# Attention stage of a four-layer kernel: context products issued in two halves around the next head's scores, and two projections of the fourth head group moved

## The reference, cut to what matters

```python
# layer 0 (A0)
scores = jnp.einsum('bkgld,bksd->bkgls', q, k) * scale
scores = scores + encoder_attention_mask[:, :, None, :, :]
attn = jax.nn.softmax(scores, axis=-1)
out = jnp.einsum('bkgls,bksd->bkgld', attn, v)
...
# layer 1 (A1 and A2)
scores = jnp.einsum('bhqd,bhkd->bhqk', q, k) / jnp.sqrt(jnp.float32(HD))
scores = scores * mask - 10000.0 * (1.0 - mask)
probs = jax.nn.softmax(scores, axis=-1)
return jnp.einsum('bhqk,bhkd->bhqd', probs, v)
```

## Time and profile before

| | us |
|---|---|
| median of 3 runs | 4186.95 |
| lowest and highest | 4186.92, 4193.72 |
| profiled execution, whole time | 4188.31 |
| its span in the trace | 4186.5 |
| span busy: PE, DVE, ACT, POOL | 89%, 63%, 51%, 39% |

### The profile page before, as it was taken

How to read it: one execution, slowest core, us unless ns; L and a number is a source line. 1 busy time by engine, 2 the same in 40 slices (tenths; PEclk the granted TensorE clock), 3 DMA queues, 4 the chain that set the end, 5 groups by cost and what they waited for, 6 DMA issues and landing times. The chain is left out here.

```text
span 4186.5 us, 66406 instructions
## 1 busy us (share of the span) xinstructions
PE 3719.4 (89%) x24448; PEld 2267.5 (54%) x24448; DVE 2621.0 (63%) x5691; ACT 2154.2 (51%) x4272; POOL 1652.4 (39%) x1849
## 2 busy tenths in 40 slices
PE   7988899899888989989888888998988888899898
PEld 4544565546554456554655445656465454565555
DVE  5765746666576564665657656467666765645766
ACT  5655733434666573343466657334346665733433
POOL 4554442232454454223245445422324544542232
PEclk9999999999999999999999999999999999999999
DMA  4032221102204122110220412211022032221102
GB/s 137 15 103 67 78 78 40 62 21 101 76 15 123 49 84 70 39 64 21 101 76 15 121 53 82 70 42 60 22 101 78 20 117 55 78 70 42 60 32 101
DMA packets 94558, 276.11 MB, mean 66 GB/s; under 512 B 25472, under 2 KB 25984, under 8 KB 73088
## 3 DMA queue, kind: packets, MB, share of 16 engines
q1 hardware_dynamic: 94208, 271.58, 20.2%
HBM read 201.24 MB, written 4.19 MB: 49 GB/s over the span
## 5 line engine op out<-in xcount | busy, mean ns | idle before, releaser
L805 POOL TENSOR_SCALAR probs<-probs,row_inv 128x512 f32<-128x512 f32 x1024 | 696.0, 696 | 635.1 <-DVE row_inv L720 635.1
L664 ACT ACTIVATE probs<-probs,row_max 128x512 f32<-128x512 f32 x1024 | 733.4, 725 | 132.1 <-DVE row_max L736 131.2
L559 PE MATMUL ps<-ident,probs 128*128 128x128 f32 x4096 | 606.5, 289 | 172.9 <-ACT pT L658 146.5
L559 PEld LDWEIGHTS ps<-ident,probs 128*128 128x128 f32 x4096 | 477.0, 146 | 383.0 <-ACT pT L658 211.4
L658 ACT ACTIVATE pT<-ps 128x512 f32<-128x512 f32 x768 | 430.1, 602 | 107.2 <-PE ps L559 106.5
L369 PE MATMUL ps<-mix,wring 128*128 128x512 f32 x1024 | 471.0, 596 | 3.8 <-DMA wring<-in_blocks_dram 3.8
L534 PE MATMUL ps<-kstack,qstack 96*128 96x512 f32 (+1 forms) x1024 | 380.5, 467 | 16.2 <-DMA qstack<-hi 7.1
L736 DVE CUSTOM_DVE_ANT_0 probs<-ps,maskA 128x512 f32<-128x512 f32 x512 | 329.3, 681 | 42.6 <-PE ps L534 42.6
L736 DVE CUSTOM_DVE_ANT_0 probs<-ps,neg 128x512 f32<-128x512 f32 x512 | 340.6, 685 | 8.9
L369 PEld LDWEIGHTS ps<-mix,wring 128*128 128x128 f32 x1024 | 191.2, 190 | 198.9 <-issue 178.8
L1535 POOL TENSOR_TENSOR hinv<-hvar,minus_half 128x32 f32<-128x32 f32 x24 | 146.3, 6094 | 376.8 <-DVE hvar L1255 376.8
(11 more groups left out here) (177 smaller groups left out, 7025.9 us busy)
## 6 DMA issues: line engine op xcount, KB each, us to landing
wring<-in_blocks_dram SPq DMA_DIRECT2D x151, 1024.0 KB, 5.1
qstack<-hi SPq DMA_DIRECT2D x256, 64.0 KB, 2.0
kstack<-hi SPq DMA_DIRECT2D x256, 64.0 KB, 2.0
maskA<-in_mask_dram SPq DMA_DIRECT2D x9, 1024.0 KB, 7.8
rows<-in_rows_dram SPq DMA_DIRECT2D x8, 1024.0 KB, 4.6
qstack<-hi SPq DMA_DIRECT2D x256, 32.0 KB, 2.0
qstack<-lo SPq DMA_DIRECT2D x128, 64.0 KB, 2.0
kstack<-lo SPq DMA_DIRECT2D x128, 64.0 KB, 2.0
```

The lines of the kernel that those rows point to most:

```text
L559: ins = nc.tensor.transpose(tile[:, qc * P:(qc + 1) * P], probs[:, m % PSLOTS, qc, kc * P:(kc + 1) * P], ident[:, :])
L664: nc.scalar.activation(p, p, ACT.Exp, bias=row_max[:, n % PSLOTS, qc:qc + 1], scale=-1.0, accum_out=row_sum[:, n % PSLOTS, qc:qc + 1]).the ...
L805: nc.gpsimd.tensor_scalar(p, p, row_inv[:, (n - 1) % PSLOTS, qc:qc + 1], 1.0, ALU.mult, ALU.mult)\
```

## The change

Three things are edited. The arithmetic stays the same.

1. In all three attentions a group's context products of key blocks 0 and 1 are issued one step earlier, behind the last transposes of the group's own last head. Those of key blocks 2 and 3 follow in the next step, behind its first scores and ahead of its transposes.
2. In A1 and A2 the query projection of group 3 moves from step 4 to steps 2 and 3, one matmul a half. It is written into bank 7, not into the ring. ACT's split of it moves to the end of step 3, POOL's with it.
3. In A1 and A2 the key projection of group 3 moves from step 5 to step 8, still in a ring bank. ACT's and POOL's splits of it move along.

The core of the diff:

```diff
+        IN_HEADS = {(0, 0): ('q', 2, (0, 1)), (0, 1): ('q', 2, (2, 3)), (1, 0): ('k', 2, (0, 1)), (1, 1): ('k', 2, (2, 3)),
+                    (2, 0): ('q', 3, (0,)), (2, 1): ('q', 3, (1,)), (3, 0): ('q', 3, (2,)), (3, 1): ('q', 3, (3,)),
+                    (8, 0): ('k', 3, (0, 1)), (8, 1): ('k', 3, (2, 3))}
+        SPLITS = {n: (kind, c) for (n, half), (kind, c, fcs) in IN_HEADS.items() if C - 1 in fcs}
...
-            tile = take(pe, 'q', A.tag, g) if tile is None else tile
+            if tile is None:
+                tile = ps[:, OBANK, :] if not A.shared and g == 3 else take(pe, 'q', A.tag, g)
...
+            def context(vg, kcs):
+
+                first, final = (vg % 2 == 0, vg % 2 == 1) if A.shared else (True, True)
+                for kc in kcs:
+                    if kc == 0:
+                        if vg == 0 and not A.shared:
+                            pe.wait_ge(*act_emptied.when('q', t, 3))
+                        if first and vg > 0:
+                            pe.wait_ge(*act_done.when('context', t, (vg // 2 if A.shared else vg) - 1))
+                        if vg == 0:
+                            for tc in range(C):
+                                pe.wait_ge(*dve_emptied.when('v', t, tc))
+                    for h in range(4):
+                        evac_wait(pe, ('pT', t, 4 * vg + h, kc))
+                    for h in range(4):
+                        lhs = v0[:, kc, vg, :] if A.shared else v1[:, kc, (4 * vg + h) * 32:(4 * vg + h + 1) * 32]
+                        ins = nc.tensor.matmul(ps[32 * h:32 * h + 32, OBANK, :], lhs, pT[:, h, kc, :],
+                                               start=(kc == 0 and first), stop=(kc == C - 1 and final))
+                    ins.then_inc(*S['context_ready'].reach(t, vg, kc))
...
-                    for kc in pair:
-                        if m >= 0 and mi == 0 and vg >= 0:
...
+                    if m >= 0 and mi == 0 and half == 0 and vg >= 0:
+                        context(vg, (2, 3))
...
-                    if not A.shared and g + 2 < A.groups and i < 2:
-                        part = (pe_q, pe_k)[i](pe, A, g + 2, fcs=(2 * half, 2 * half + 1), tile=None if half == 0 else part)
+                    if m >= 0 and mi == 3 and half == 1:
+                        context(mg, (0, 1))
+
+                    if not A.shared and (n, half) in IN_HEADS:
+                        kind, c, fcs = IN_HEADS[n, half]
+                        part = {'q': pe_q, 'k': pe_k}[kind](pe, A, c, fcs=fcs, tile=None if 0 in fcs else part)
...
+            bank = OBANK if label[0] == 'q' and not A.shared and g == 3 else ring.bank(*label)
...
-                    if step == 's' and not A.shared and g + 2 < A.groups and i < 2:
-                        act_split(act, A, 'qk'[i], g + 2)
+                    if step == 's' and not A.shared and n in SPLITS:
+                        act_split(act, A, *SPLITS[n])
...
+                if not A.shared and n - 2 in SPLITS:
+                    pool_split(pool, A, *SPLITS[n - 2])
```

More of the change, by code:

```diff
@@ L521, in pe_attention @@
                 vg = mg - 1
-                first, final = (vg % 2 == 0, vg % 2 == 1) if A.shared else (True, True)
                 if n < A.heads and i == 0:
@@ L536, in pe_attention @@
                                 .then_inc(*S['scores_ready'].reach(t, n, qc))
-                    for kc in pair:
-                        if m >= 0 and mi == 0 and vg >= 0:
-                            if kc == 0:
-                                if first and vg > 0:
-                                    pe.wait_ge(*act_done.when('context', t, (vg // 2 if A.shared else vg) - 1))
-                                if vg == 0:
-                                    for tc in range(C):
-                                        pe.wait_ge(*dve_emptied.when('v', t, tc))
-                            for h in range(4):
-                                evac_wait(pe, ('pT', t, 4 * vg + h, kc))
-                            for h in range(4):
-                                lhs = v0[:, kc, vg, :] if A.shared else v1[:, kc, (4 * vg + h) * 32:(4 * vg + h + 1) * 32]
-                                ins = nc.tensor.matmul(ps[32 * h:32 * h + 32, OBANK, :], lhs, pT[:, h, kc, :],
-                                                       start=(kc == 0 and first), stop=(kc == C - 1 and final))
-                            ins.then_inc(*S['context_ready'].reach(t, vg, kc))
+                    if m >= 0 and mi == 0 and half == 0 and vg >= 0:
+                        context(vg, (2, 3))
                     if 0 <= m < A.heads:
@@ L623, in act_split @@
             bias = scaled[:, t * C + g:t * C + g + 1] if kind == 'q' else col(A.bk, g)
-            nc.scalar.activation(split[:, s, :], ps[:, ring.bank(*label), :], ACT.Identity, bias=bias,
+            bank = OBANK if label[0] == 'q' and not A.shared and g == 3 else ring.bank(*label)
+            nc.scalar.activation(split[:, s, :], ps[:, bank, :], ACT.Identity, bias=bias,
                                  scale=A.scale if kind == 'q' else 1.0).then_inc(*act_emptied.reach(*label))
@@ L796, in pool_attention @@
                 g, i = divmod(n - 1, 4)
-                if not A.shared and g + 2 < A.groups:
-                    if i == 1:
-                        pool_split(pool, A, 'q', g + 2)
-                    if i == 2:
-                        pool_split(pool, A, 'k', g + 2)
+                if not A.shared and n - 2 in SPLITS:
+                    pool_split(pool, A, *SPLITS[n - 2])
                 for qc in range(C):
```

## The result

The changed kernel takes **4201.91 us** (median), the kernel before 4186.93 in the same rounds. The ratio is 1.0031, 95% interval 1.0021 to 1.004: slower by 15 us, where no change was forecast. The time lies inside the stated range (4168 to 4203), at its slow end. The profiled execution took 4201.91 us with a span of 4200.1, against a span of 4186.5 before.

What follows compares the result with a forecast made beforehand. No engine is full, so hand-over waits between engines bound the kernel. A0 +5.0, A1 and A2 -8.1, stack +1.6 sum to -1.5 us: 4185.4 median, forecast as no change, range 4168 to 4203.

Steps and rivals of the forecast that it cites:

- X + 6.04: A1 and A2: X starts ACT's copies in a group's last step; next head's copy follows a context at X + 6.04.
- A0, 7 x 4 groups at 0.18: A0's context steps: second copy 0.18 us later in each of 28 groups, +5.0 us in all.
- a run under 6.8: Sign against the forecast: a solid PE run in A0 shorter than 6.8 us means its idle time was reached.
- Chain, point 1: A1: ACT's copies of step 4 at 282.43, step 6 at 288.47, step 7 at 293.69, 3.25 us earlier than before.
- Chain, points 2 and 3: A1: key split included, copies at 304.44, 1.97 us gain left; second context's second copies at 312.85, 1.34 left.
- Rival D: The move does nothing, the ring's wait only moving from step 5 to 9: 4187 us; inside the forecast's shared 58%.
- Chain, point 4: A1: third context to 333.58 against 334.59, leaving 1.0 us gained in each of eight attentions, -8.1 in all.
- rival B: A1 and A2: DVE's 0.9 us wait adds to ACT's at each context, 21.6 us more, 4207 us; 12%.
- The stack, 0.4 late: A2: group 3's key stack, behind the load of o2, lands 0.4 us late for step 12, four times: +1.6 us.
- DVE's waits: A1: DVE still waits for late scores around the contexts, about 3 us in all, beside ACT's wait.
- Rival C: The clock falls into a context once a sample and attention, 8 x 2 to 3.7 us more: 4201 to 4215; 5%.
- The rule weighed in the prediction: PE's clock, all stretches: idle gaps make it fall and work after them runs at half rate; no size given.

Runs made afterwards that it cites:

- the weights late: A2's output-weight load issued behind group 3's stack: against the changed kernel 4198.89 us; against the kernel with only the query and key projections moved 4166.76 us.
- the two fastest kernels: Query and key projections moved, contexts at old places, A2's output weights loaded behind the stack: 4166.76 us; with group 3's key tile also in the context bank: 4161.18 us.
- projections alone: The changed kernel with the contexts back at their old places, so only the query and key projections of group 3 move: 4180.73 us, ratio 0.9984.

## Why the forecast of no change was wrong

The forecast failed in the chain of A1 and A2, on the price of a halved context. It put the next head's copy at X + 6.04; the trace has X + 6.31, X + 6.73 and X + 6.35. At the third context A1 is then 0.5 us behind the kernel before, where it was to be 1.0 ahead: 1.5 us in each of 8 attentions, 12 of the 15.1 us between the forecast and the profiled execution (the samples without a low stretch in these parts agree within 0.02 us). The stack of A2 is the second miss, with 1.3 us for 0.4. By the prediction's own steps:

- **A0, 7 x 4 groups at 0.18.** Right in its mechanism. First copy predicted at 107.38 by before's clock, measured 108.07 less 0.68 of shift, 107.39; second at 108.58, measured 109.27 - 0.68 = 108.59. The term came out at 7.1 us for 5.0, 0.25 a group: the delay of the exponentials isn't taken up, and the reciprocals' wait grows from 0.31 to 0.59 us. What stood as a criterion, a run under 6.8, was met by 0.03 without its meaning: the transposes in one piece take 1.93 for 2.05.
- **Chain, point 1: the step that failed first.** X itself is right: 282.43 predicted, 283.85 - 1.37 = 282.48 measured. The next copy was to come at 288.47 and comes at 290.16 - 1.37 = 288.79; step 7's at 293.69 and come at 294.01. The sum took its pieces from a step without a context: the last four transposes start at X + 0.63, take 0.41, and the scores take 0.54. At the third context, X = 327.73, the rows have X + 0.70, 0.59 and 0.66, and the copy at X + 6.35. 0.3 for each of 24 contexts is 7 us. The 1.21 us of step 5 were gone, as forecast.
- **Chain, points 2 and 3: a wait left out, and a dearer split.** Step 9's copies were predicted at 304.44 and come at 304.95, since the key split costs ScalarE 1.48 us for 1.29. In step 9 the ring lacks the bank of the key tile, TensorE stands 1.22 us, and its transposes come in one late lump: the context starts at X + 1.67, for the 1.04 predicted, and the copy lies at X + 6.73. The second pair of copies, predicted at 312.85, comes at 315.43 - 1.37 = 314.06. Rival D named exactly this wait ("only moves from step 5 to 9") and the sum left it out. It is worth 0.4 to 0.6 for each attention, 3 to 5 us.
- **Chain, point 4.** The second pair behind the third context was to come at 333.58 and comes at 336.47 - 1.37 = 335.10, for 334.59 before. That is the sign that was set for rival B.
- **The stack, 0.4 late.** Mis-sized, and not by its arrival. The issue began 446.37 - 437.78 = 8.6 us behind the copies of A2's step 7, for 443.0 - 434.5 = 8.5 in the sum; the 24 DMAs took 15.9 for 15.1, one group of four 3.25. By the sum's rule the scores of step 12 had to start by 464.2 (4.73 behind the copies at 460.67, less 1.24), and they start at 464.25. But they and the transposes run at the lower clock: 1.02 us from scores to transposes for 0.54, and 1.10 from there to the copy for 0.70, so this comes at 466.37 for 465.4. The part of A2 with it measures 2.01, 1.3 more than the same part in A1 or than with the weights late: 5 us for 1.6. A low stretch lies in this part in three of four samples with the weights late too, and costs nothing there, so by these rows it takes both.
- **DVE's waits** were to be some 3 us in A1, beside ScalarE's. The trace has 3.4 us in six pieces, none over 0.8, so rival B, which set 0.9 on top of each of three contexts, isn't what happened, though its sign was right.
- **Rival C** (the clock falls into a context, 5%) was given too little. In A2's part between first and second copy two samples of four had a low stretch, and lost 1.5 and 0.4 us; at the stack all four had one.

That the change came out slower rests on both sides of it. By the prediction's own numbers the halved contexts cost 5.0 us in A0 and 8.41 - 7.78 = 0.63 for each of 24 in A1 and A2, or 20 in all, and were measured at 21 to 25; what is left of the forecast's -1.5, some -22 for the projections, was measured at -6.5. With the ring's and the stack's waits mended the projections are worth -25.7 (4161.18 less 4186.83).

The balance over the eight attentions, measured less predicted: to the first copy +2.6 (-2.9 for -3.25 each), first to second copy +8.4 (2.97 for 1.92), second to third +6.3 (0.63 for 0.34 in A1; 2.01 for 0.74 in A2), third to fourth -3.4, A0 +2.1, the rest -1.1: 14.9, of the 15.1 between the forecast -1.5 and the profiled 13.6. The -3.4 is the clock's, as the last section shows: no term of the forecast has it, and in the profiled execution it hides as much of the loss. The median lies 1.1 us inside the range, which is no merit of the working, since that misses by 16.5. What remains open is why the stretch between A0 and A1 got shorter, which is part of the 2.6.

## What to carry to other kernels

A piece of work that is moved needs idle time on its engine within the same hand-over cycle, so count how much of it stands in each gap between two groups of the instructions that others wait for. Here one half of a context in each of two gaps was the cheaper order; both halves in one gap cost 0.6 to 1.1 us more for each context of A1 and A2. If a bank's hold is moved, look for the wait at its new place before booking the gain, and for what stands behind it. And when a producer is moved later, follow the queue that carries its result: here one weight load issued ahead of a stack was worth 12 to 14 us with the contexts at their old places, twice the gain that the move itself had, and 3 us with them halved.

## What the hardware showed

TensorE's granted clock falls to 0.50 in the rows below, behind slices in which the engine had waited for much of the time (0.20 and 0.74 of 1.50 us busy in two of the three ahead of it here). After the change, at step 8 of A2 (from:to, length, busy us by engine, PEclk, DMA share, GB/s):

```profile
1484.00:1485.50 1.50, 0.20 (x2) 0.12 (x2) 1.47 (x5) 1.50 (x5) 0.92 (x2) 1.00 0.00 0
...
1487.00:1488.50 1.50, 0.74 (x4) 0.75 (x5) 1.50 (x6) 1.50 (x5) 0.25 (x1) 0.81 0.00 0
1488.50:1490.00 1.50, 1.50 (x4) 0.71 (x3) 1.47 (x4) 1.50 (x6) 1.11 (x2) 0.50 0.00 0
1490.00:1491.50 1.50, 1.50 (x4) 0.65 (x2) 0.69 (x5) 1.50 (x5) 1.31 (x2) 0.55 0.00 0
```

That is the lower of its two levels, 1.2 GHz. What such a stretch costs depends on where it falls. A2 between first and second copy in two samples of the changed kernel with the weights late, the same instructions with it (from 3.7 us behind the first copy, in the step with the key projection) and without:

```profile
1485.80:1510.20 24.40, 20.78 (x120) 12.67 (x120) 20.61 (x49) 21.13 (x53) 12.13 (x18) 0.93 0.25 60
2535.70:2558.60 22.90, 19.18 (x120) 11.87 (x120) 20.60 (x49) 20.91 (x53) 12.15 (x18) 1.00 0.26 64
```

1.5 us, and 1.5 too at that place in the two fastest kernels (23.32 for 21.83, 22.75 for 21.25). In the kernel with halved contexts in A1 and A2 alone, which has no projection in this step, the part is 21.05 us with a stretch from 3.7 and without one: nothing. In the kernel before it has 20.10 us at a clock of 1.00 and 20.60 at 0.92, with the stretch from 8.3:

```profile
2525.80:2545.90 20.10, 16.04 (x114) 10.36 (x112) 19.86 (x48) 19.70 (x50) 10.55 (x16) 1.00 0.45 125
3567.60:3588.20 20.60, 17.34 (x115) 11.76 (x113) 20.26 (x49) 19.75 (x52) 10.93 (x16) 0.92 0.51 138
```

The part from third to fourth copy has no halved context and no projection, and is the same in every kernel. Without a low stretch it takes 12.4 us, with one of 3.4 us that starts 5.2 to 6.4 us behind the third copy 13.2 to 13.7. In A2 the kernel before has a stretch from 5.2 us or later in all four samples and the change in none, which gives it 1.0 to 2.4 us in each; in A1 the change has one there in all four. The samples of one kernel differ in it: with the projections alone one A2 has none and three have one there.

A0's beginning is another such place. From its first scores to its first copy it takes 48.9 us in each sample of before, and 50.3 in each sample of projections alone, whose A0 has the same instructions; with the weights late as well, two samples have the one and two the other. The clock is down for 6.8 us there, or for 10.2, as in the first sample of projections alone:

```profile
49.30:59.50 10.20, 10.20 (x36) 7.93 (x37) 8.50 (x27) 8.27 (x21) 6.16 (x10) 0.50 0.16 54
```

That is 5.6 us of a profiled run that no edit made, so times of single runs are compared only by parts, and kernels by their medians.

Over A1 and A2 in four samples, each from its first scores to its fourth copy, 17 low stretches lie before the change and 23 after; with the projections alone it is 23 as well, and that kernel is faster all the same. So their number isn't what decides, but the place. The rule weighed in the prediction, "TensorE: Matmul & The Clock Gate" of the Trainium skill (section HAM oscillation), agrees with these rows in that the fall follows waits.
